# A new start for the first two tiles of a gated attention block, and the casts of x and context moved from DVE to ACT

## What is computed

```python
def instance_norm(a): # over the 512 columns
    ...
qp = Wq @ instance_norm(layernorm(x)) + bq
kp = Wk @ instance_norm(ctx) + bk
sp = Ws @ ctx + bs_
attn = softmax(einsum('bcn,bcm->bnm', qp, kp), axis=-1)
mean = attn @ sp ;  mean_sq = attn @ (sp * sp)
x = x + tanh(g_xattn) * (instance_norm(ctx) * sqrt(relu(mean_sq - mean**2)) + mean)
w = (weight_q - 8) * scales + zeros # by groups of 128
x = x + tanh(g_ffn) * (layernorm(x) @ w.T)
```

## Time and profile before

| | us |
|---|---|
| median of 3 runs (lowest, highest) | 186.06 (185.04, 186.35) |
| the profiled execution | 186.42 |
| its span, first to last instruction | 184.6 |
| outside the span | 1.8 |
| busy: PE / DVE / ACT / POOL | 167.2 / 141.0 / 118.0 / 120.4 |

### The profile page before, as it was taken

One profiled execution on the slowest core, in us unless ns is written; L12 is line 12 of the kernel. 1 busy time (PEld: TensorE's weight loads), 2 busy tenths in 40 slices (PEclk: granted clock), 3 DMA queues, 4 the chain that ended last, 5 costly groups with the idle time before them and its releaser, 6 DMA issues.

```text
span 184.6 us, 3489 instructions
## 1 busy us (share of the span) xinstructions
PE 167.2 (91%) x1128; PEld 147.1 (80%) x1128; DVE 141.0 (76%) x311; ACT 118.0 (64%) x261; POOL 120.4 (65%) x145
## 2 busy tenths in 40 slices
PE   1554999999999999999999999999999979789992
PEld 0432889999999999999999999998789867567881
DVE  2897696689859887986988798676159679988851
ACT  2253575978598678859867885995569995232110
POOL 1455586917955896799589679944328959966310
PEclk9999999999999999999999999999999999999999
DMA  6408566883796699679679966356100000111212
GB/s 169 166 21 202 186 159 138 237 201 86 184 319 153 155 287 245 162 216 286 139 170 249 283 145 153 78 134 151 44 0 0 4 0 0 57 62 60 111 57 114
DMA packets 14321, 25.75 MB, mean 139 GB/s; under 512 B 2336, under 2 KB 2464, under 8 KB 14304
## 3 DMA queue, kind: packets, MB, share of 16 engines
q1 hardware_dynamic: 14304, 25.54, 52.2%
HBM read 9.67 MB, written 2.10 MB: 64 GB/s over the span
## 4 chain that ended last, share of the span: by engine, by line
PE 76%; DVE 9%; ACT 4%; issue 4%; POOL 3%; DMA 2%; SPq 0%; ACTq 0%; POOLq 0%
PE pv_bank L322 28%; PE turn_bank L306 14%; PE score_bank L296 8%; PE score_bank L297 8%; PE side_bank L333 3%; PE score_bank L377 3%; PE score_bank L371 3%; PE score_bank L370 3%; DVE X L667 2%; DMA CTX<-in_context 2%; PE side_bank L342 2%; ACT probs L442 1%; PE side_bank L283 1%; DVE result L692 1%; DVE stats L673 1%
## 5 line engine op out<-in xcount | busy, mean ns | idle before, releaser
L831 POOL TENSOR_SCALAR probs<-probs,rden 128x512 f32<-128x512 f32 x64 | 50.9, 796 | 32.2 <-DVE rden L623 32.0
L322 PE MATMUL pv_bank<-probs_t,values 128*128 128x128 f32 x512 | 67.7, 276 | 0.0
L442 ACT ACTIVATE probs<-score_bank,neg_max 128x512 f32<-128x512 f32 x64 | 44.1, 690 | 31.4 <-DVE neg_max L616 30.8
L322 PEld LDWEIGHTS pv_bank<-probs_t,values 128*128 128x128 f32 x512 | 62.4, 192 | 2.1 <-issue 1.7
L616 DVE TENSOR_REDUCE neg_max<-score_bank 128x1 f32<-128x512 f32 x64 | 43.5, 682 | 15.0 <-PE score_bank L297 14.4
L306 PE MATMUL turn_bank<-ident,probs 128*128 128x128 f32 x256 | 38.8, 275 | 1.1 <-ACT probs_t L450 1.0
L450 ACT COPY probs_t<-turn_bank 128x512 f32<-128x512 f32 x64 | 37.1, 581 | 3.2 <-PE turn_bank L306 3.0
L306 PEld LDWEIGHTS turn_bank<-ident,probs 128*128 128x128 f32 x256 | 31.1, 142 | 5.7 <-POOL probs L831 1.1
L296 PE MATMUL score_bank<-c_both,q_both 128*128 128x512 f32 x64 | 29.3, 458 | 2.3 <-ACT q_with_x L494 2.3
L297 PE MATMUL score_bank<-c_with_bias,q_with_x 128*128 128x512 f32 x64 | 26.4, 412 | 0.0
L296 PEld LDWEIGHTS score_bank<-c_both,q_both 128*128 128x128 f32 x64 | 13.0, 202 | 4.6 <-issue 2.9
(11 more groups left out here) (99 smaller groups left out, 243.6 us busy)
## 6 DMA issues: line engine op xcount, KB each, us to landing
c_both<-c_hi SPq DMA_DIRECT2D x30, 128.0 KB, 2.6
X<-in_x SPq DMA_DIRECT2D x8, 256.0 KB, 3.0
CTX<-in_context SPq DMA_DIRECT2D x8, 256.0 KB, 4.1
ctx_now<-in_context SPq DMA_DIRECT2D x8, 256.0 KB, 2.9
sz<-in_scales_zeros SPq DMA_DIRECT2D x4, 512.0 KB, 6.7
out<-result SPq DMA_DIRECT2D x8, 256.0 KB, 2.0
q_with_x<-x_hi SPq DMA_DIRECT2D x15, 128.0 KB, 2.3
c_with_bias<-c_lo SPq DMA_DIRECT2D x15, 128.0 KB, 2.9
```

The lines of the kernel that those rows point to most:

```text
L322: last = pe.matmul(pv_bank[b][:, P * j:P * j + P], values[t % 2][:, i, b, :, :].rearrange("p a c -> p (a c)"), probs_t[g % PROBS_T][:, P * ...
L442: act.activation(probs[g % PROBS][:, :], score_bank[g % SBANKS][:, :], ACT.Exp, bias=neg_max[:, c:c + 1], accum_out=den[:, c:c + 1]).then_ ...
L831: pool.tensor_scalar(probs[g % PROBS][:, :], probs[g % PROBS][:, :], rden[:, c:c + 1], 1.0, ALU.mult, ALU.mult).then_inc(probs_done, 1)
```

## The change

1. **Start of tile 0.** The context is loaded first and x second, and the parameters by a DMA that ACT issues. x is not split: q of tile 0 is one fp32 product (`project_first`) of the unsplit A (`w_a`) and the unsplit normalised x, in 128 columns to one bank and then 384 to another, so that scores(0) needs the first 128 alone. High and low parts of q for the first batch are written straight to their stacked rows; for the second batch POOL, ACT and DVE write half of the rows and four DMAs carry the other half. A is split on POOL, later.
2. **Tile 1.** project(1) moves from in front of scores(3) to after turn(2); its x cast, context normalisation, c_lo and so on move into the first chunks. value_product(0) moves behind turn(0). project(2) moves from chunk 7 to chunk 8, and statistics, normalisation and splitting of tile 2 to chunks 4 to 7.
3. **Casts.** x_hi and c_hi of tiles 1 to 7 are cast by ACT (`cast_x_hi`, `cast_c_hi`) in place of DVE.

```diff
+            sp.dma_start(CTX[:, 0, :], context_tiles[0]).then_inc(first_loaded[0][1], DMA)
             sp.dma_start(X[:, 0, :], x_tiles[0]).then_inc(first_loaded[0][0], DMA)
-            sp.dma_start(params_sb[:, :], params).then_inc(params_loaded, DMA)
-            sp.dma_start(CTX[:, 0, :], context_tiles[0]).then_inc(first_loaded[0][1], DMA)
             load(1, *first_loaded[1])
             load_ctx_now(0)
+            sp.wait_ge(first_c_both, 3)
+            sp.dma_start(c_both[1][0:C, :] ..., c_both[1][C:P, :] ...)
+            sp.wait_ge(first_q_hi, 4)
+            sp.dma_start(q_both[1][0:C, :] ..., q_hi[0][C:P, :] ...)
+            sp.dma_start(q_with_x[1][0:C, :] ..., q_hi[0][C:P, :] ...)
             sp.wait_ge(c_lo_done, 1)
-            stack(0, 1, *x_and_context_copies)
-            sp.wait_ge(q_lo_done, 1)
-            stack(0, 1, *q_copies)
+            sp.dma_start(c_with_bias[1][0:C, :] ..., c_lo[0][C:P, :] ...)
...
+            def project_first():
+                pe.wait_ge(xn_done, 1)
+                pe.wait_ge(w_a_ready, 1)
+                pe.matmul(turn_bank[1][:, FIRST], w_a[:, :], xn[:, FIRST], start=True, stop=True)
+                pe.matmul(side_bank[:, REST], w_a[:, :], xn[:, REST], start=True, stop=True)
...
             multiply_weights()
-            pe.wait_ge(w_split, 1)
-            project(0)
-            pe.wait_ge(bias_rows_ready, 2)
-            for g in range(AHEAD_S):
+            project_first()
+            for g in range(AHEAD_S + 1):
                 scores(g)
-            pe.wait_ge(q_lo_done, 1)
-            project(1)
-            scores(AHEAD_S)
-            value_product(0)
...
+                    if g == CHUNKS:
+                        pe.wait_ge(s_kept, 2)
+                        project(2)
                     turn(g)
+                    if g == 0:
+                        value_product(0)
+                    if g == 2:
+                        project(1)
...
+            def cast_x_hi(t):
+                act.wait_ge(xn_done, t + 1)
+                if t >= 3:
+                    act.wait_ge(stacked[0], STACK * (t - 2))
+                    act.wait_ge(stacked[1], STACK * (t - 2))
+                act.copy(x_hi[t % 2][:, :], xn[:, :]).then_inc(x_hi_cast, 1)
+            def cast_c_hi(t):
+                act.wait_ge(ctxn_done, t + 1)
+                act.copy(c_hi[t % 2][:, :], CTX[:, t, :]).then_inc(c_hi_cast, 1)
...
+                    if g == 0:
+                        cast_x_hi(1)
+                    if g == 1:
+                        cast_c_hi(1)
+                    if g == 6:
+                        cast_x_hi(2)
+                    if g == 7:
+                        cast_c_hi(2)
+                    if c == 4 and 1 <= t and t + 2 < TILES:
+                        cast_x_hi(t + 2)
+                    if c == 6 and 1 <= t and t + 2 < TILES:
+                        cast_c_hi(t + 2)
...
+            x_statistics(1)
+            first_lo(2, 0, side_bank, REST, q_both[0])
+            maximum(0)
+            ctx_statistics(1)
+            maximum(1)
+            reciprocal(0)
+            finish_statistics(1)
+            maximum(2)
+            reciprocal(1)
+            first_lo(3, 1, turn_bank[1], FIRST, q_hi[0])
+            first_lo(4, 1, side_bank, REST, q_hi[0])
             normalise_x(1)
-            keep_x_hi(1)
```

More of the change, by code:

```diff
@@ L190, in rows_of, with x_hi_of, c_hi_of @@
             return slice(C * b, C * b + C)
+        def x_hi_of(engine, t):
+            engine.wait_ge(x_hi_cast, t)
+        def c_hi_of(engine, t):
+            engine.wait_ge(c_hi_cast, t)
         def values_bank(t):
@@ L486, in _ @@
[L486 to L494 removed]
+            act.wait_ge(ctxn_done, 1)
@@ new lines, in _ @@
+            act.copy(c_both[0][0:C, :], CTX[0:C, 0, :]).then_inc(first_c_both, 1)
+            act.wait_ge(w_multiplied, 1)
+            act.copy(w_a[:, :], pv_bank[1][:, 0:P]).then_inc(w_a_ready, 1)
+            act.copy(c_both[0][C:P, :], CTX[0:C, 0, :]).then_inc(first_c_both, 1)
+            act.wait_ge(b_ready, 1)
+            act.wait_ge(first_q_done, 1)
+            act.activation(q_both[0][0:C, FIRST], turn_bank[1][0:C, FIRST], ACT.Identity,
+                           bias=b_a[0:C, 0:1]).then_inc(first_q_hi, 1)
@@ L704, in _ @@
-            dve.tensor_copy(b_a[:, :], pv_bank[1][:, P:P + 2]).then_inc(b_ready, 1)
-            normalise_ctx(0)
-            dve.tensor_copy(q_with_x[0][C:P, :], x_hi[0][0:C, :].bitcast(F32)).then_inc(stacked[0], DMA)
-            keep_c_hi(0)
-            dve.wait_ge(c_hi_done, 1)
-            dve.tensor_tensor(c_with_bias[0][0:C, :], CTX[0:C, 0, :], c_hi[0][0:C, :].bitcast(F32),
-                              ALU.subtract).then_inc(stacked[0], DMA)
-            dve.wait_ge(q_hi_done, 1)
-            dve.scalar_tensor_tensor(q_both[0][C:P, :], side_bank[0:C, :], b_a[0:C, 0:1],
-                                     q_hi[0][0:C, :].bitcast(F32), ALU.add, ALU.subtract).then_inc(stacked[0], DMA)
@@ L720, in _ @@
             dve.wait_ge(gates_ready, 1)
-            for g in range(AHEAD_S):
-                maximum(g)
-                if g > 0:
-                    reciprocal(g - 1)
-            normalise_ctx(1)
-            keep_c_hi(1)
             for t in range(TILES):
@@ L887, in _ @@
             pool.tensor_copy(c_with_bias[1][C:P, :], b_a[C:P, 1:2].broadcast_to([C, N])).then_inc(bias_rows_ready, 1)
+            pool.wait_ge(xn_done, 1)
             pool.wait_ge(bias_rows_ready, 2)
-            split_c_lo(0)
-            inverse_deviation(1)
-            pool.memset(averages[:, :], 1.0 / N).then_inc(consts_ready, 1)
-            split_x_lo(1)
-            for g in range(AHEAD_E):
-                normalise_probs(g)
-            split_c_lo(1)
+            pool.tensor_copy(q_with_x[1][C:P, :], xn[C:P, :]).then_inc(second_x_rows, 1)
+            pool.wait_ge(first_c_both, 3)
+            pool.wait_ge(second_x_rows, 1)
+            pool.tensor_tensor(c_lo[0][C:P, :], CTX[C:P, 0, :], c_both[1][C:P, :].bitcast(F32),
+                               ALU.subtract).then_inc(c_lo_done, 1)
+            pool.wait_ge(w_a_ready, 1)
+            pool.wait_ge(c_lo_done, 1)
+            pool.tensor_copy(w_a_hi[:, :], w_a[:, :]).then_inc(w_a_hi_ready, 1)
+            pool.wait_ge(w_a_hi_ready, 1)
+            pool.tensor_tensor(w_a_lo[:, :], w_a[:, :], w_a_hi[:, :].bitcast(F32), ALU.subtract).then_inc(w_split, 1)
+            normalise_probs(0)
+            inverse_deviation(1)
+            normalise_probs(1)
             for t in range(TILES):
```

259 lines of the change are left out of this document (164 added, 95 removed).

## The result

The change makes the kernel slower by 0.9%: 187.69 us (187.53 to 187.84, four runs) against 186.20 (185.04 to 186.62, four runs) on the same chip, ratio 1.0086 with a 95% interval of 1.0045 to 1.0127. The profiled execution took 187.7, its span 185.9; before 186.42 and 184.6. So 1.3 us more stand inside the span.

What follows compares the result with a forecast made beforehand. PE's work was taken to bound the middle, so only the time before PE is never short of work could pay. Profiled 186.42, less 1.6 at chunk 8, plus 0.4 after it, gave 185.2, or 184.8 against the median; range 182.9 to 187.4.

Steps and rivals of the forecast that it cites:

- The start of tile 0: Start of tile 0: x at 5.0, xn ready at 7.5, first scores at 9.6, 2.6 us earlier.
- The chain of tile 1: Tile 1's stack: c_lo at 22.4, landing 28.6; chunk 8 starts then in place of 30.19, 1.6 us gained.
- The main step: Ahead of chunk 8: its scores wait for the stack DMAs; an earlier PE eats up the stack's 2.9 us reserve.
- I let DVE wait and then keep POOL off.: Tile 1's context normalisation on DVE during POOL's x_lo: DVE waits, then keeps POOL off for 0.45 us.
- After chunk 8: "0.4 us lost": Chunk 8 to exp(10): with two more casts on ACT, PE loses 0.4 us waiting for exp(10); bounds nothing and 1.2.
- The clock hardly matters.: Ahead of chunk 8: with the clock risen 3 us earlier or later, PE still comes before or about 28.6.
- The rival in which the clock falls in the wait: PE's 2.5 us stop ahead of chunk 8 lowers the clock, costing 3.1 us: 187.9; chance 0.08.
- The casts in the middle, at nothing: Tiles 2 to 7, chunks 4 and 6: ACT's idle time holds the casts at no cost; otherwise 0.6 us each.
- The rival of ACT behind in every tile: One cast in each of six tiles lengthens PE's tile by 0.62 us, 3.7 in all: 188.5; chance 0.05.
- The sum: Whole kernel: profiled execution 186.42, less 1.6, plus 0.4, gives 185.2; against the median 184.8.

Runs made afterwards that it cites:

- the fastest kernel: Changed kernel with tile 1's stack DMAs issued piece by piece, tile 2's casts on DVE and tile 1's squares on POOL in chunk 5: 182.63 us, ratio 0.9826.
- early stack: Changed kernel with each of tile 1's seven stack DMAs issued when its source is ready, c_lo's last: 184.32 us, ratio 0.9887.
- preparation moved forward: Changed kernel with tile 2's statistics, normalisations, casts and splits in chunks 4 and 5: 186.89 us alone; 185.90 with 26 filler transposes ahead of chunk 8.
- the casts alone: Kernel before the change, with only the casts of tiles 2 to 7 moved to ACT in chunks 4 and 6: 186.12 us, ratio 1.0017.
- the long filler: Changed kernel with 26 transposes of the identity on PE ahead of chunk 8's scores: 188.45 us, ratio 1.0119.

## Why the prediction was wrong

- **The start of tile 0.** Right within 0.4 us. xn was ready at 7.62 (7.5), the first scores started at 9.55 (9.6) and the second at 11.29 (10.9). x was there by 5.08 (5.0). Context came at 4.06, not 3.5, without effect.
- **The chain of tile 1.** Right. xn of tile 1 ended at 15.70 (16.6), c_lo ended at 21.77 (22.4), SP issued from 21.79 to 25.52, 3.73 us, and the landing took 2.4. Chunk 8 started at 27.98, 28.6 foretold; PE was there at 25.45 (26.1), not quite unbroken from 13.98 on, but with the high clock early; PE waited 2.53, 2.5 foretold. The main step, by which an earlier PE is worth only the stack's reserve, stood.
- **"I let DVE wait and then keep POOL off."** The mechanism is real and was placed wrong: for tile 1 it cost 0.2 us (x_lo 1.44, c_lo 1.29) and not 0.45, and after chunk 8, where the sum had nothing, 0.7 for tile 2's xn. There and in the fastest kernel xn ended 0.28 us after the POOL instruction that had begun just ahead of it (33.21 against 32.93; 30.05 against 29.77). (The Trainium skill, SBUF — State Buffer, section "SBUF: two separate sides", says that whichever of such two starts first holds the shared ports for its whole instruction; these rows agree.)
- **After chunk 8: "0.4 us lost".** This is the step that failed; it measured 3.5, of which 1.6 are PE at half speed and 1.9 gaps of PE. With the clock high (early stack) the gaps alone are 3.0: 1.0 for x_lo, 1.2 for the variance, the rest in gaps of 0.4 and less. Three parts of the step were off. It followed the cast as far as the exponential of chunk 10, put its end at +8.8, and stopped. The trace has it start at +9.3 (37.28) and end at about +10, and five operations follow it in line (q_hi, q_lo, statistics, the maximum of chunk 12, the variance) before PE weighs chunk 8 at +14.1. It took xn at 0.54 where POOL's squares made it 1.25, and gave x_lo behind it no wait at all. And it took scores and turns from 28.6 on at full speed.
- **"The clock hardly matters."** True ahead of chunk 8, where it was argued: the step was 0.23 us as early as 11.3, and chunk 8 waited for its DMAs just the same. False behind it. The rival in which the clock falls in the wait had its mechanism right and got a chance of 0.08. Its price was 3.1; 1.6 us of slow work were seen, of which 1.0 (preparation moved forward) or 0.5 (nothing else changed) came back in d when the clock was held up. The price came from a rise after 6.25 us without a gap; here the high level was back some 4 us after PE had started again.
- **The casts in the middle, at nothing.** Right: a tile is 15.98 us of PE work with 13.56 on ACT, and the casts alone changed nothing. The rival of ACT behind in every tile is out.
- **The sum.** 186.42, less 2.2 at chunk 8, plus 3.5 after it: 187.7. With 0.4 for the last term it would have been 184.6. The general error is one of kind: the reserve of PE was priced, and what the new order does to tile 2's reserve on DVE, ACT and POOL was not. Its normalisation moved from 2.96 us ahead of chunk 8's scores to 3.98 behind them. The prediction had it there (done at +4.05), but followed only ACT's two casts from it, and not what x_lo, q_lo and the variance then wait for.

What stays open: why chunk 8's stack came up to 1.7 us later in some kernels of the same order of DMAs (from 27.98 to 29.73), enough to hide half of what an experiment removed. The rows show where, not why: SP's issue of c_lo's DMA, the fourth of the seven, takes 0.60 us in the changed kernel and in the one with the preparation moved forward, and 1.36 to 2.05 in six others, with a filler and without. What makes it long was not tried. So a difference of up to 1.5 us between two single profiles can be this issue alone. Nor was it controlled when in the start the clock first rises: PE's step is 0.23 from 11.3 us on in some profiles and only from about 16.5 in others.

## What to carry to other kernels

A start that runs ahead into a fixed DMA wait buys only the slack of that wait. Price such a change three times: what PE loses in the stop, what clock PE has afterwards, and, stop or no stop, which work of the next tile, though ready, the new order has put behind the first instruction that waits for PE. Then cut the wait at its source. Issuing each piece of the stack when its own source was ready took the kernel from 0.9% slower to 1.1% faster than before, with the two casts of the late chain put back to 1.5% faster, and with the squares moved too to 1.7%. When two paths run side by side, removing one can show little (the long filler took 0.5 off d and nothing off the time); remove both before dropping either.

## What was unexpected of the hardware

The granted clock falls after a stop of PE of this size. The columns are those of the earlier trace rows; PE stood still from 25.45 to 27.98, and the three microseconds from 28 read 0.50 (above). With a stop of 2.1 us it fell too. In kernels with the long filler, where PE had worked on transposes up to a stop of 0.6 or 1.2, it read 1.00 throughout. In the kernel with the preparation moved forward, PE stopped for 2.8 us and went on at 28.56, and these are its stretches:

```profile
28.00:29.00 1.00, 0.44 (x2) 0.40 (x3) 0.00 (x0) 1.00 (x2) 0.93 (x1) 1.00 0.88 195
29.00:30.00 1.00, 1.00 (x8) 0.83 (x7) 0.67 (x2) 0.67 (x3) 1.00 (x2) 0.90 0.94 215
30.00:31.00 1.00, 1.00 (x6) 1.00 (x6) 0.81 (x4) 0.95 (x3) 1.00 (x2) 0.50 0.94 217
31.00:32.00 1.00, 1.00 (x7) 1.00 (x6) 0.03 (x1) 0.99 (x3) 1.00 (x2) 0.50 0.84 191
32.00:33.00 1.00, 1.00 (x7) 1.00 (x6) 0.00 (x0) 0.00 (x0) 0.93 (x2) 0.50 0.25 64
```

Here PE worked more than a microsecond at 1.00 before the clock dropped to 0.50: the fall comes late, over work that has already begun, and a look at the first matmul behind a stop does not show it. (The Trainium skill, TensorE: Matmul & The Clock Gate, section "HAM oscillation", tells of waits for a next slice that put the clock down; the traces agree for stops of 2.1 us and more.) After the later waits of the changed kernel, 1.2 us at the most, PEclk stayed at 1.00.
